# A graph attention kernel: E and the normed rows turned by VectorE blocks and DMAs instead of TensorE

## The chip, the cores and the metric

One NeuronCore of one Trainium2 chip runs the whole kernel. The metric is the device time of one execution in microseconds. The kernel before took 1281.48 us as the median of three runs (1281.45 to 1281.96).

## The reference, cut to what matters

64 graphs of 128 nodes with 256 features. The input is layer-normed and clipped at zero, goes through three layers of attention over the graph's edges and a feed-forward network, and the input is added at the end.

```python
h = maximum(layernorm(x), 0)
for l in range(3):
    si = h @ attn_w[l, :256];  sj = h @ attn_w[l, 256:]
    scores = si[:, :, None] + sj[:, None, :] + attn_b[l]
    scores = where(scores >= 0, scores, 0.2 * scores)
    scores = where(mask, scores, -inf)            # mask = adjacency or the diagonal
    agg = einsum('bij,bjd->bid', softmax(scores), h)
    h = layernorm(h + agg, g1[l], beta1[l])
    ff = gelu(h @ W1[l] + b1[l]) @ W2[l] + b2[l]  # 256 -> 1024 -> 256
    h = layernorm(h + ff, g2[l], beta2[l])
return x + h
```

## The kernel before

**Items.** Four graphs make a group, there are 16 groups, and one layer of one group is an item: 48 items. They run in rounds of 12: layer 0 of four groups, layer 1 of the same four, layer 2. In an item, partitions are the 128 nodes, and the free dimension holds 4 graphs of 256 features (`xs`, a ring of three). The four graphs' nodes make 512 columns in the feed-forward network.

**Orders written by hand.** Each engine has a list of steps for the first items and a function `slot(s)` for the rest, which places the steps of several items: f = item s, b = s+1, a = s+2, d = s+3, p = s+4, t = s-1, o = s-2. Engines run their lists in order and wait on semaphores. DMAs are all issued by SP, in its own order.

**An item's path, by the names in the code.** Attention: `j_dots` and `i_dots` (VectorE, L606 and L624) make sj and si; sj goes to DRAM and comes back broadcast to all partitions (`send_sj`, `load_sj`) with the element order node, graph, so that one graph's row is read with 16 bytes between elements; `masked` (L645) takes the minimum of it and a penalty; `leaky` (ScalarE, L838) adds si and applies the slope; `minus_max` (VectorE, L656) reduces to the negated maximum; `exps` (ScalarE, L844) makes E, with its row sums. TensorE turns E with four transposes (`e_turn`, L993) into the PSUM tile `util`, ScalarE copies it to `ET` (`et_out`, L851), and `aggregate` (L962) multiplies: eight halves of fp32 matmuls, ET being the weights. `attend` (VectorE, L660) divides by the sum and adds the rows. `moments1`, `make_rstd("1")` (GpSimd) and `norm1` (VectorE, L677) norm them. TensorE turns the normed rows with 2 x 4 transposes (`z1_turn`, L980) into `util`, `h_high` (ScalarE, L832) applies gain and offset and rounds, `h_low` (VectorE, L683) keeps the rest.

Feed-forward: `ffn1(i, c)` (L930) makes chunk c of eight of the hidden rows, six matmuls of 512 columns into one of three PSUM banks (`hbank`): it needs `low` of three chunks before. `gelu_high(i, c)` (ScalarE) applies gelu and rounds, `low(i, c)` (VectorE, L538) keeps the rest in one of four buffers, `ffn2(i, c)` (L944) adds 12 matmuls of 256 columns to `acc`. `residual` (L544), `moments2`, `norm2` and, on GpSimd, `x_gamma` and `x_beta` make the next layer's rows. `h_gamma` and `h_beta` (GpSimd) make the residual's rows `hb`.

**PSUM.** Eight banks: three `hbank`, four `acc` (an item's two halves, for two items in turn; both aggregate and ffn2 write them, L138), one `util`, which e_turn and z1_turn hand round with et_out and h_low.

**Inputs.** During the items in front of a new layer 0 VectorE also takes the moments of the next input (`input_moments`, `input_shift`), ScalarE norms it (`first_x`), and VectorE makes the penalty.

Of the kernel before, what the change touches and what calls it, by code (L numbers as in the profile page):

```python
# [25 lines left out]
F32 = mybir.dt.float32  # L26
# [7 lines left out]
P = 128  # L34
GG = 4
# [11 lines left out]
LEAD = 3  # L47

# [3 lines left out]
def build(nc, x, adj, attn_w, attn_b, W1, b1, W2, b2, g1, beta1, g2, beta2, out):  # L52
# [19 lines left out]
    with ExitStack() as ctx:  # L72
# [27 lines left out]
        ET = sb("ET", [P, GG, P])  # L100
        sj_bc = sb("sj_bc", [P, P, GG])
        sj_dram = nc.dram_tensor("sj_dram", [2, P, GG], F32).ap()
# [8 lines left out]
        dots = sb("dots", [P, 2, GG])  # L111
        si = sb("si", [P, GG])
# [4 lines left out]
        nmr0 = sb("nmr0", [P, GG])  # L117
        st = {n: sb(f"st{n}", [P, GG, 6]) for n in "012"}
        mv = {n: sb(f"mv{n}", [P, GG, 2]) for n in "012"}
        ve = {n: sb(f"ve{n}", [P, GG]) for n in "012"}  # L120
        rstd = {n: sb(f"rstd{n}", [P, GG]) for n in "012"}
# [13 lines left out]
        acc = [psum(f"acc{i}", [P, HG, D]) for i in range(4)]  # L135
        util = psum("util", [P, TOK])

        def acc_of(i, h): return acc[2 * (i.q % 2) + h]  # L138
# [28 lines left out]
        zt_n = sem("zt_n")  # L167

# [13 lines left out]
        si_n = sem("si_n")  # L182
        pen_n = sem("pen_n")
        mask_n = sem("mask_n")
        negm_n = sem("negm_n")
        rden_n = sem("rden_n")
        nmr0_n = sem("nmr0_n")
        st_n = {n: sem(f"st{n}_n") for n in "012"}
# [30 lines left out]

        def x_of(i):  # L220
            return xs[:, i.q % XR]
# [28 lines left out]

        def wait_ring(eng, q):

            if q >= XR:
                eng.wait_ge(zt_n, KD * (q - XR + 1))
                eng.wait_ge(hgam_n, 2 * (q - XR + 1))
# [3 lines left out]
        def _(sp):  # L259
# [36 lines left out]
            def load_weights(n):  # L296
                l, w, h = halves[n]
# [4 lines left out]
            def send_sj(i):  # L302
                sp.wait_ge(dotj_n, i.q + 1)
                wait(sp, sj_in, 16 * (i.q - 2))
                sp.dma_start(sj_dram[i.q % 2], dots[:, 1]).then_inc(sj_sent, 16)

            def load_sj(i):
                sp.wait_ge(sj_sent, 16 * i.q)
# [3 lines left out]

            def slot(s):
                t, o, d, p = item(s - 1), item(s - 2), item(s + 3), item(s + 4)
                if p and p.l == 0:
                    load_xraw(p)
                if 6 <= s + 5 < len(halves):
                    load_weights(s + 5)
                if s == ITEMS - 4:
                    sp.wait_ge(x0_n, GG * NG)  # L320
                    sp.dma_start(xraw[:], group(x, NG - 1)).then_inc(last_in, 16)
                if o and o.l == L - 1 and o.q < ITEMS - 1:
                    for h in range(2):
                        gs = slice(h * HG, (h + 1) * HG)
                        sp.wait_ge(out_ready, 2 * o.g + h + 1)
                        sp.dma_start(group(out, o.g)[:, gs], xout[:, o.g % 2, gs]).then_inc(out_sent[o.g % 2], 16)
                if t and t.l == L - 1 and t.q < ITEMS - 1:
                    wait(sp, out_ready, 2 * t.g)
                    if t.g == 0:
                        sp.wait_ge(ln1_ready, 1)  # L330
                    sp.dma_start(xres[:], group(x, t.g)).then_inc(xres_in, 16)
                if p and p.l == 0:
                    load_adj(p)
                if d:
                    send_sj(d)
                    load_sj(d)

            load_xraw(item(0))
# [10 lines left out]
            load_xraw(item(2))  # L349
            load_adj(item(1))  # L350
            load_ln2_rows()
            load_attn_rows(False)
            load_weights(4)
            send_sj(item(1))
            load_sj(item(1))
            load_adj(item(2))
            load_weights(5)
            load_adj(item(3))
            load_xraw(item(3))
            send_sj(item(2))  # L360
# [747 lines left out]
```

## Time and profile before

| | us |
|---|---|
| median of three runs | 1281.48 |
| the profiled execution | 1281.6 |
| its span, first to last instruction | 1279.8 |
| TensorE busy | 1240.6 (97% of the span) |
| VectorE busy | 1110.3 (87%) |
| ScalarE busy | 917.7 (72%) |
| GpSimd busy | 652.5 (51%) |
| DMA engines | 14.4% of the span, mean 41 GB/s |

TensorE's granted clock is 0.997 of 2.4 GHz over the span. In the profile PE is TensorE's matmuls, PEld its weight loads, DVE VectorE, ACT ScalarE, POOL GpSimd, SPq the queue from which SP issues DMAs. Matmuls overlap, so the distance between two starts tells what one costs, not its duration.

### The profile page before, as it was taken

How to read it: one execution, taken by the hardware profiler on the slowest of the kernel's cores; microseconds unless marked ns; L12 is line 12 of the kernel's file. 1: busy time of each engine (PE TensorE's matmuls, PEld its weight loads, DVE VectorE, ACT ScalarE, POOL GpSimd, SP SyncE). 2: the span in 40 equal slices, each digit the busy share in tenths (PEclk: the TensorE clock that was granted, in tenths of full speed). 3: DMA queues.
4: the chain of work that ended last, by engine and by line, in shares of the span. 5: the costliest groups of instructions: out<-in, count | busy, mean ns of one | idle time of the engine just before them, and what ended most of it. 6: DMA issues, size and time to landing. Idle time of an engine off the chain costs nothing.

```text
span 1279.8 us, 23042 instructions
## 1 busy us (share of the span) xinstructions
PE 1240.6 (97%) x7877; PEld 1122.5 (88%) x7877; DVE 1110.3 (87%) x3331; ACT 917.7 (72%) x1754; POOL 652.5 (51%) x535
## 2 busy tenths in 40 slices
PE   3899999999999999999999999999999999999997
PEld 1799999988899999999889999999989899989996
DVE  7888888899998788889998888789999888888765
ACT  4777777677876776678777776777778766776663
POOL 1435553556555534554566445544666355435563
PEclk9999999999999999999999999999999999999998
DMA  7111111112220001011230000002321100000111
GB/s 248 53 33 43 26 26 34 34 51 66 67 67 10 10 10 17 10 34 51 75 100 26 9 18 10 9 10 43 99 75 42 34 10 9 10 17 26 26 41 58
DMA packets 52944, 52.31 MB, mean 41 GB/s; under 512 B 9272, under 2 KB 45148, under 8 KB 52828
## 3 DMA queue, kind: packets, MB, share of 16 engines
q1 hardware_dynamic: 52828, 50.85, 14.4%
q8 instruction: 62, 1.02, 0.3%
q14 instruction: 54, 0.44, 0.1%
HBM read 42.36 MB, written 8.48 MB: 40 GB/s over the span
## 4 chain that ended last, share of the span: by engine, by line
PE 77%; DVE 18%; ACT 2%; issue 2%; DMA 1%; POOL 0%; DVEq 0%; POOLq 0%
PE acc L955 35%; PE hbank L940 33%; PE acc L969 5%; DVE hid_lo L541 3%; PE util L990 3%; DVE xs L680 2%; PE util L1000 1%; DVE xs L667 1%; DVE st L528 1%; DVE st L674 1%; DVE ve L519 1%; DVE mv L517 1%; DVE st L562 1%; DVE junk L627 1%; DVE sc L654 1%
## 5 line engine op out<-in xcount | busy, mean ns | idle before, releaser
L955 PE MATMUL acc<-w2hi,hid_hi 128*128 128x256 f32 x1536 | 446.0, 290 | 0.0
L813 ACT ACTIVATE hbank<-hbank,vec 128x512 f32<-128x512 f32 x384 | 253.7, 661 | 266.5 <-PE hbank L940 262.0
L955 PE MATMUL acc<-w2hi,hid_lo 128*128 128x256 f32 x1536 | 434.9, 283 | 0.0
L955 PE MATMUL acc<-w2lo,hid_hi 128*128 128x256 f32 x1536 | 434.4, 283 | 0.0
L389 POOL TENSOR_TENSOR rstd<-ve,halfs 128x4 f32<-128x4 f32 x111 | 120.1, 1082 | 492.1 <-DVE ve L519 487.2
L940 PE MATMUL hbank<-ht_hi,w1hi 128*128 128x512 f32 x768 | 311.2, 405 | 2.8 <-DVE hid_lo L541 1.4
L955 PEld LDWEIGHTS acc<-w2hi,hid_hi 128*128 128x128 f32 x1536 | 293.8, 191 | 10.5
L940 PE MATMUL hbank<-ht_lo,w1hi 128*128 128x512 f32 x768 | 302.6, 394 | 0.0
L955 PEld LDWEIGHTS acc<-w2lo,hid_hi 128*128 128x128 f32 x1536 | 293.7, 191 | 8.8
L940 PE MATMUL hbank<-ht_hi,w1lo 128*128 128x512 f32 x768 | 300.8, 392 | 0.0
L955 PEld LDWEIGHTS acc<-w2hi,hid_lo 128*128 128x128 f32 x1536 | 293.5, 191 | 0.0
L541 DVE TENSOR_TENSOR hid_lo<-hbank,hid_hi 128x512 fp32r<-128x512 f32 x384 | 257.5, 683 | 26.5 <-ACT hid_hi L819 24.7
L819 ACT CAST hid_hi<-hbank 128x512 fp32r<-128x512 f32 x384 | 225.6, 587 | 13.7 <-PE acc L955 1.7
L409 POOL TENSOR_TENSOR hb<-xs,ln_rows 128x512 f32<-128x512 f32 x96 | 128.9, 1343 | 87.2 <-DVE xs L680 87.2
L940 PEld LDWEIGHTS hbank<-ht_hi,w1lo 128*128 128x128 f32 x768 | 144.7, 188 | 32.6
L940 PEld LDWEIGHTS hbank<-ht_hi,w1hi 128*128 128x128 f32 x768 | 145.7, 190 | 25.6 <-DVE ht_lo L685 2.1
L940 PEld LDWEIGHTS hbank<-ht_lo,w1hi 128*128 128x128 f32 x768 | 145.9, 190 | 19.9
L685 DVE TENSOR_TENSOR ht_lo<-util,ht_hi 128x512 fp32r<-128x512 f32 x96 | 66.2, 689 | 95.1 <-ACT ht_hi L836 95.1
L416 POOL TENSOR_TENSOR hb<-hb,ln_rows 128x512 f32<-128x512 f32 x96 | 124.5, 1298 | 0.0
L680 DVE TENSOR_SCALAR xs<-xs,mv,rstd 128x256 f32<-128x256 f32 x192 | 112.0, 646 | 1.0 <-POOL rstd L389 0.9
L829 ACT ACTIVATE util<-util,vec 128x512 f32<-128x512 f32 x96 | 72.4, 754 | 36.1 <-PE util L990 35.9
L426 POOL TENSOR_TENSOR xs<-xs,ln_rows 128x512 f32<-128x512 f32 x64 | 82.7, 1292 | 23.4 <-DVE xs L570 23.4
(76 smaller groups left out, 1740.3 us busy)
## 6 DMA issues: line engine op xcount, KB each, us to landing
sj_bc<-sj_dram SPq DMA_DIRECT2D x47, 256.0 KB, 3.9
xraw<-in_x_dram SPq DMA_DIRECT2D x16, 512.0 KB, 4.4
out_dram<-xout SPq DMA_DIRECT2D x32, 256.0 KB, 4.4
xres<-in_x_dram SPq DMA_DIRECT2D x15, 512.0 KB, 5.6
xout<-in_L_gnn_W_dram SPq DMA_DIRECT2D x10, 512.0 KB, 5.0
adji<-in_adj_dram SPq DMA_DIRECT2D x16, 256.0 KB, 2.9
ln_rows<-in_L_gnn_g_dram SPq DMA_DIRECT2D x2, 384.0 KB, 8.0
ln_rows<-in_L_gnn_beta_dram SPq DMA_DIRECT2D x2, 384.0 KB, 7.6
```

The costliest lines, as they stand in the source:

```text
L389: pool.tensor_tensor(rstd[n][:], ve[n][:], halfs[:], ALU.pow).then_inc(rstd_n[n], 1)
L409: pool.tensor_tensor(hb[:, i.q % 2, gs], x_of(i)[:, gs], rows_of(ln1_rows[:, 0], i.l), ALU.mult).then_inc(hgam_n, 1)
L416: pool.tensor_tensor(t, t, rows_of(ln1_rows[:, 1], i.l), ALU.add).then_inc(hb_n, 1)
L426: pool.tensor_tensor(t, t, rows_of(ln2_rows[:, 0], i.l), ALU.mult).then_inc(gam_n, 1)
L541: dve.tensor_tensor(hid_lo[:, k % HID], hbank[k % HB][:], hid_hi[:, k % HID].bitcast(F32), ALU.subtract).then_inc(lo_n, 1)
L680: dve.tensor_scalar(x_of(i)[:, g], x_of(i)[:, g], mv["1"][:, g, 0:1], rstd["1"][:, g:g + 1], ALU.subtract, ALU.mult).then_inc(z1_n, 1)
L685: dve.tensor_tensor(ht_lo[:, i.q % 2, m], util[:], ht_hi[:, i.q % 2, m].bitcast(F32), ALU.subtract).then_inc(htlo_n, 1)
L813: act.activation(hbank[k % HB][:], hbank[k % HB][:], ACT.Gelu, bias=b1c(i.l, c)).then_inc(gelu_n, 1)
L819: act.copy(hid_hi[:, k % HID], hbank[k % HB][:]).then_inc(hi_n, 1)
L829: act.activation(util[:], util[:], ACT.Identity, bias=beta1c(i.l, m), scale=g1c(i.l, m)).then_inc(ht_n, 1)
L940: mm = pe.matmul(hbank[k % HB][:], w[:, i.l, m, at_c], v[:, i.q % 2, m], start=m == 0 and n == 0, stop=m == KD - 1 and n == 2)
L955: mm = pe.matmul(to, v[:, k % HID, of_g], w[:, i.l, c], start=c == 0 and n == 0 and g % HG == 0, stop=c == C - 1 and n == 2, skip_group_ch ...
```

## The change

For all items but the first two, E is turned by one VectorE operation that transposes blocks of 32x32 in place of the four TensorE transposes (`turn_e`), written to DRAM (`send_e`) and read back by four DMAs that put the blocks in their places (`move_e`); the normed rows likewise (`turn_z`, `send_z`, `move_z`), so `h_out` reads the SBUF tile `zt`. Pieces are 512 bytes. `ET` has the graph as its innermost dimension, so aggregate reads its weights with 16 bytes between elements. norm1 goes from VectorE to ScalarE, with its shift made by VectorE (`shift1`). minus_max no longer reduces E's scores: masked, now one operation for each graph, returns the maximum, from which two operations on 128x4 make the exponent's offset. add_bias goes (the offset is the start value of i_dots), input_shift is one operation instead of four, the variance's small operation goes to GpSimd. Aggregation gets two banks of its own (`mix`), ffn2 two (`acc`). All lists of steps are in another order; aggregate(a), for one, stands ahead of ffn1(b,0) instead of behind ffn1(b,2).

```diff
-        acc = [psum(f"acc{i}", [P, HG, D]) for i in range(4)]
+        acc = [psum(f"acc{i}", [P, HG, D]) for i in range(HG)]
+        mix = [psum(f"mix{i}", [P, HG, D]) for i in range(HG)]
...
+            def send_e(i):
+                if i.q < BY_PE:
+                    return
+                sp.wait_ge(te_n, moved(i.q))
+                wait(sp, et_in, MOVES * (moved(i.q) - 1))
+                sp.dma_start(e_dram, te[:].rearrange("p b t g -> p (b t g)")).then_inc(e_sent, 16)
+
+            def move_e(i):
...
+                sp.wait_ge(e_sent, 16 * moved(i.q))
+                sp.wait_ge(agg_n, 2 * i.q)
+                for b in range(NQ):
+                    sp.dma_start(ET[b * QD:(b + 1) * QD].rearrange("p a t g -> p a (t g)"),
+                                 e_dram.rearrange("(a p) (b f) -> b p a f", a=NQ, b=NQ)[b]).then_inc(et_in, 16)
+
+            def send_z(i):
...
+                sp.dma_start(z_dram, tz[:].rearrange("p c g t -> p (c g t)")).then_inc(z_sent, 16)
+
+            def move_z(i):
...
+                sp.wait_ge(z_sent, 16 * moved(i.q))
+                sp.wait_ge(ht_n, KD * i.q)
+                for b in range(NQ):
+                    sp.dma_start(zt[b * QD:(b + 1) * QD].rearrange("p m a g t -> p m a (g t)"),
+                                 z_dram.rearrange("(a p) (m b f) -> b p m a f", a=NQ, b=NQ, m=KD)[b]).then_inc(zt_in, 16)
...
# SP's slot
+                if b:
+                    send_z(b)
+                if a:
+                    send_e(a)
+                if b:
+                    move_z(b)
+                if a:
+                    move_e(a)
+                if t and t.l == L - 1:
+                    load_xres(t)
+                if o and o.l == L - 1:
+                    send_out(o, 1)
+                load_weights(s + 6)
+                if d:
+                    send_sj(d)
+                    load_sj(d)
...
# VectorE
-                dve.tensor_tensor(sc[:], pen[:, i.g % PENS], row, ALU.min).then_inc(mask_n, 1)
+                for g in range(GG):
+                    last = dve.tensor_tensor_reduce(sc[:, g], pen[:, i.g % PENS, g], row[:, g], 1.0, -BIG, ALU.add,
+                                                    ALU.max, msj[:, g:g + 1])
+                last.then_inc(mask_n, 1)
...
+            def turn_e(i):
...
+                dve.transpose(te[:].rearrange("p b i g -> p b g i"), sc[:].rearrange("p g (b j) -> p b g j", j=QD)).then_inc(te_n, 1)
+
+            def turn_z(i):
...
+                dve.transpose(tz[:], x_of(i).rearrange("p g (c j) -> p c g j", j=QD)).then_inc(tz_n, 1)
...
# ScalarE
+            def norm1(i):
+                act.wait_ge(nmr1_n, i.q + 1)
+                for g in range(GG):
+                    act.activation(x_of(i)[:, g], x_of(i)[:, g], ACT.Identity, bias=nmr1[:, g:g + 1],
+                                   scale=rstd["1"][:, g:g + 1]).then_inc(z1_n, 1)
...
# TensorE
-                    pe.wait_ge(y1_n, GG * (i.q + 1))
+                    wait(pe, y2_n, 2 * i.q)
...
-                    mm = pe.matmul(acc_of(i, h)[:, g % HG], ET[:, g], x_of(i)[:, g],
+                    mm = pe.matmul(mix_of(i, h)[:, g % HG], ET[:].rearrange("p a i g -> p (a i) g")[:, :, g], x_of(i)[:, g],
```

The new orders of a slot, by the names of the steps (those with p only where p is of layer 0, add_input, load_xres and send_out only for layer 2):

```
TensorE: ffn1(f,3) ffn2(f,0) ffn1(f,4) ffn2(f,1) ffn2(f,2) ffn1(f,5) ffn1(f,6) ffn2(f,3) ffn2(f,4) ffn1(f,7)
         aggregate(a,0) aggregate(a,1) ffn2(f,5) ffn1(b,0) ffn1(b,1) ffn2(f,6) ffn2(f,7) ffn1(b,2)
VectorE: turn_z(b) moments2(t) low(f,2) turn_e(a) input_moments(p) norm2(t,0) norm2(t,1) low(f,3) penalty(p)
         low(f,4) low(f,5) low(f,6) input_shift(p) j_dots(d) h_low(b,0) i_dots(d) attend(a,0) h_low(b,1)
         attend(a,1) moments1(a) low(f,7) masked(d) low(b,0) minus_max(d) shift1(a) low(b,1)
         residual(f,0) residual(f,1)
ScalarE: gelu_high(f,2) exps(a) gelu_high(f,3..6) h_high(b,0) h_high(b,1) gelu_high(f,7) first_x(p)
         gelu_high(b,0) gelu_high(b,1) leaky(d) norm1(a)
GpSimd:  h_gamma(b,1) make_rstd("2",t) make_rstd("0",p) x_gamma(t,0) x_beta(t,0) x_gamma(t,1) add_input(t,0)
         x_beta(t,1) make_rstd("1",a) h_beta(f,1) h_beta(b,0) add_input(t,1) h_gamma(a,0)
```

## Rows read from the trace of the kernel before

**Rows 1.** Busy time of each engine by stretch: start:end, length, busy, clock, DMA.
```profile
61.13:1270.11 1208.98, 1205.91 (x7721) 1096.00 (x7720) 1055.31 (x3141) 880.76 (x1680) 632.80 (x511) 1.00 0.13 35
...
sum 1279.80, PE 1240.58 PEld 1122.45 DVE 1110.27 ACT 917.72 POOL 652.54; mean PE 310.14 PEld 280.61 DVE 277.57 ACT 229.43 POOL 163.14
```

**Rows 2.** The chain of waits in order of time, one item: start, us, what.
```profile
502.75 2.75 PE hbank L940 x12
505.50 0.44 PE util L1000 x4
...
507.33 1.73 PE acc L969 x8
...
520.31 0.44 PE util L990 x4
...
524.01 4.32 PE acc L955 x36
```

**Rows 3.** Busy time by stretch (PE, PEld, DVE, ACT, POOL), two items.
```profile
509.28:534.86 25.58, 25.58 (x167) 23.29 (x166) 21.36 (x65) 18.25 (x35) 12.49 (x11) 1.00 0.08 11
...
637.18:662.76 25.58, 25.17 (x163) 22.68 (x162) 25.28 (x78) 19.57 (x39) 15.78 (x13) 1.00 0.28 80
```

**Rows 4.** VectorE's instructions in order of time: start, us, line, operation.
```profile
509.12 1.66 DVE L667 SCALAR_TENSOR_TENSOR xs<-acc,rden,xs 128x256 f32<-128x256 f32 x4
510.70 0.73 DVE L570 TENSOR_SCALAR xs<-xs,mv,rstd 128x256 f32<-128x256 f32 x2
511.34 0.69 DVE L541 TENSOR_TENSOR hid_lo<-hbank,hid_hi 128x512 fp32r<-128x512 f32 x1
511.94 1.40 DVE L674 BATCH_NORM_STATS2 st<-xs 128x6 f32<-128x256 f32 x4
...
513.79 0.29 DVE L519 TENSOR_SCALAR ve<-mv 128x4 f32<-128x4 f32 x1
...
515.24 1.10 DVE L654 TENSOR_TENSOR sc<-pen,sj_bc 128x512 f32<-128x512 bf16 x1
516.26 2.35 DVE L680 TENSOR_SCALAR xs<-xs,mv,rstd 128x256 f32<-128x256 f32 x4
```

**Rows 5.** ScalarE's instructions in order of time.
```profile
500.21 1.28 ACT L848 ACT_TABLE_LOAD   x1
501.51 0.41 ACT L848 ACTIVATE sc<-sc,negm 128x128 f32<-128x128 f32 x1
...
503.18 1.28 ACT L813 ACT_TABLE_LOAD   x1
...
505.17 0.59 ACT L819 CAST hid_hi<-hbank 128x512 fp32r<-128x512 f32 x1
...
520.79 0.75 ACT L829 ACTIVATE util<-util,vec 128x512 f32<-128x512 f32 x1 [0.59 <-PE util L990]
521.57 0.59 ACT L836 CAST ht_hi<-util 128x512 fp32r<-128x512 f32 x1
522.05 1.28 ACT L842 ACTIVATE sc<-sc,si 128x128 f32<-128x128 f32 x4
```

**Rows 6.** Groups by line (count, busy us, mean ns), and one instruction of ScalarE.
```profile
L969 PEld LDWEIGHTS acc<-xs,ET 128*128 128x128 f32 x384 | 73.6, 192 | 13.4 <-ACT ET L854 1.9
...
L510 DVE TENSOR_TENSOR w1lo<-xout,w1hi 128x1024 fp32r<-128x1024 f32 x6 | 7.3, 1218 | 0.7 <-ACT w1hi L808 0.7
...
L654 DVE TENSOR_TENSOR sc<-pen,util 128x512 f32<-128x512 bf16 x1 | 0.7, 683 | 0.0
...
610.34 2.09 ACT L862 ACTIVATE xs<-xraw,nmr,rstd 128x256 f32<-128x256 f32 x4
```

**Rows 7.** DMAs: KB, median us to landing; landing of out_dram; issue ns.
```profile
adji<-in_adj_dram SPq DMA_DIRECT2D x16, 256.0 KB, 2.9
...
DMA to landing us min/median/max: 2.1/4.4/5.7
...
L305 SPq DMA_DIRECT2D sj_dram<-dots x47: 319/320/339, 26.5 to 1196.7; - x47
```

## What I expect of the change

> **What bounds the kernel now.** I read the busy time by stretch first: from 61.13 to 1270.11 us TensorE is idle for 3.07 us only, and over the whole span it is busy 1240.58 of 1279.80 us, so 39.2 us of idle time lie almost wholly at the two ends [rows 1]. Then the chain of waits in order of time: in the steady part it runs through TensorE alone, without a wait [rows 2]. One item takes a period of 25.58 us: 8 chunks of the first product (2.75 us for two, so 1.38 each), 8 of the second (4.32 us for three, 1.44 each), one aggregation (1.73), and three groups of four transposes at 0.44 us, one for E and two for the normed rows [rows 2]. Then the busy time per item: VectorE has 21.4 of 25.58 us in most items, but 25.3 of 25.58 in the items during which the next inputs are also normed; there TensorE loses 0.4 us [rows 3]. So what TensorE saves is time saved, as long as VectorE (in four items of each twelve it is full) and the chains through the other engines let it.
>
> **What goes from TensorE.** For 46 of 48 items (the first two keep them) 3 x 0.44 = 1.32 us of transposes go: the period falls to 24.26 us, and 46 x 1.32 = 60.7 us in all. The profiled execution took 1281.6 us, 1.8 over its span, and agrees with the median of 1281.48. So the floor is 1281.6 - 60.7 = 1220.9 us, if nothing else stalls and the two ends stay as they are.
>
> **VectorE.** Out go: norm1, four operations in 2.35 us, where the same operation in norm2 takes 0.73 for two [rows 4] (so about 0.8 us of it is waiting beside GpSimd); the reduction for the maximum (512 elements, as the 0.6 us of low) becomes two operations of four elements; the tensor_scalar of the variances (0.29) twice or three times, and add_bias, of the same size [rows 4]. That is 2.35 + 0.6 + 0.6 + 0.2 = 3.8 us. In come two block transposes, of 512 and 1024 elements a partition. No row shows a block transpose on VectorE. Nearest are low (512 elements, 0.60 from start to start) and the 1024-element subtraction (1.22) [rows 4, 6]; from above I take twice these. A gain is excluded, since the operations are new. I take 0.8 + 1.2 = 2.0, near the lower end, since other operations here go by element count and only the write of the small one is strided; the upper end is 3.6. masked becomes four operations with an accumulator read: its strided form took 1.10 against 0.68 with a dense operand [rows 4, 6], and three more starts make it 1.3, between 1.1 and 2.0. shift1 and the two small operations of minus_max come to 0.6. Net: -3.8 + 2.0 + 0.2 + 0.6 = -1.0 us (up to +1.3 by the upper ends). A normal item has 20.4 of 24.26 us, an item with inputs about 24.3 of 24.26. VectorE is therefore the bound in the latter.
>
> **ScalarE** gets norm1, four operations in 2.09 us like first_x [rows 6], and loses the 0.6 us copy of E. It has 18.3 to 19.6 us an item now [rows 3], so some 21 of 24.26: room, but its place in the queue counts. GpSimd gets the small variance operations; at 12.5 to 15.8 us [rows 3] it has room.
>
> **The new chains.** Set zero at the start of ffn1(f,3) in a slot. The bound is the loop that starts when aggregate(a) ends at 15.8: reciprocal and half of attend (0.95), h_low (0.6), other half (0.8), moments1 (1.85), low (0.6), masked (1.3) on VectorE; leaky (1.28), norm1 (2.1) on ScalarE: 9.5 us. Behind norm1 in ScalarE's queue stand gelu_high (1.3), a table load, exps, a table load (1.28 + 1.67 + 1.28), gelu_high again (1.3), then low(f,3) (0.6): 7.4 us. Only then may ffn1(f,6) start, since three PSUM banks carry the hidden rows; to the next end of aggregate it is 1.38 + 2.88 + 1.38 + 1.73 = 7.4 us [rows 2, 4, 5]. Sum 24.3, with four handovers of up to 0.1 us 24.3 to 24.7, against 24.26 for TensorE. I take 24.4: +0.15 us in 34 normal items, 5 us. norm1 so ends 1.0 us into the next slot; behind it turn_z ends at 2.2, exps at 5.3 (1.0 + 1.3 + 1.28 + 1.67), turn_e at 6.1, low(f,3) at 8.3. In the 12 items with inputs, input_moments (1.85, like moments1) now stands between turn_e and norm2 in front of low(f,3): turn_e ends at 6.1, then 1.85, norm2 1.3, low 0.6: 9.9 instead of 8.3. With the 0.15 that is 1.7 us each, 20 us. attend, penalty, the moved dots and the merged shift lie elsewhere and are hidden by waits for gelu or for aggregate.
>
> **The own banks.** Aggregation gets two banks and ffn2 two instead of four taken in turn. ffn2(f,0) then waits for residual of the item before, which by the same clock ends at about 24.8, 0.5 us into the slot, and is wanted at 1.38. The 0.9 us of slack hides it; in items with inputs some 0.7 is left. The PSUM tile that et_out and the transposes held is no longer handed round.
>
> **E by DMA.** turn_e ends near 6.1, aggregate wants E at 14.1: 8.0 us. SP must write 256 KB (landing in 2.1 to 5.7 us, the least when nothing is in flight), then issue four pieces at 0.32 to 0.4 us each, the last of which lands like adji (256 KB in pieces of 512 bytes, 2.9) [rows 7]: 2.6 + 1.1 + 2.8 and some 0.2 for waits = 6.7. Hidden by 1.3 us. **The normed rows.** turn_z ends near 2.2; 512 KB out in 3.5, then four issues and the landing of 512 KB: 3.5 + 1.1 + 3.3 = 7.9, but send_e is queued ahead of move_z on SP and waits for turn_e until 6.1, so they are there at about 10.6; ScalarE turns to h_high at 11.3, when gelu_high(f,6) is done (ffn1(f,6) ends at 9.8). If they came later, h_high (0.75 + 0.59 for each half [rows 5]) with h_low between could start at 13.7 before ffn1(b,0) waits. On SP send_z and send_e now wait ahead of weights, xres and send_sj; send_sj wants its dots at 13 us, when SP has gone past, and load_sj is in before masked wants it at 20.
>
> **E's layout.** ET is now read as weights with 16 bytes from one element to the next. No row shows TensorE reading so. VectorE does in masked: 0.42 us more for 512 elements, 0.8 ns each [rows 4, 6]. Eight loads of 128 would cost 0 to 0.82 us an item. I take 0: a load takes 192 ns and a matmul of the aggregation 1.73 / 8 = 216 ns [rows 2, 6], loads run beside matmuls, and 0.1 us more for each may just fit. 
>
> **The start** is reordered: j_dots(i1) comes earlier, but aggregate(i2) must now go in front of ffn1(i0,7), with a DMA trip of its own. The first lets it pass two weight splits (1.22 each [rows 6]), attend and moments1 of i0, some 6 us; the second costs at most its trip, 6.7. I take 0, and ±6 for the range.
>
> **Sum:** 1220.9 + 5 + 20 = 1246 us.
>
> **The rivals.**
> 1. *The strided weights show.* Then 0.82 us an item on the loop, 46 x 0.82 = 38: 1284 us, no change within 0.2%. For it: masked's price. Against: the loads' cover. 0.08.
> 2. *VectorE is the bound everywhere*: block transposes at the upper ends put turn_z at 2.4 and turn_e at 1.2 in front of low(f,3), which comes 0.6 us later in every item: 46 x 0.6 = 28, 1274 us. For it: nothing but the lack of a row. 0.15. The Trainium skill (VectorE: DVE Perf Modes, Rules for kernel authors) advises TensorE for a 128x128 transpose whose result may be in PSUM, and 311 ns on VectorE for a bf16 one (The three transpose paths); twelve make 3.7 us, an estimate, which is this rival. No run here shows it.
> 3. *The DMA trips become the loop, and it is slower than before.* The trip of the normed rows has 11.5 us before ffn1 waits, from 2.2 to 13.7. Nearest rows from above are 5.7 us for 256 KB out, so up to 8.5 for 512, and 6.8 back with the issues: 15.3, which is 3.8 too long each item: 1246 + 175 = 1421 us. It decides from 11.5 us; from 12.3 it is slower than before (0.8 x 46 = 36). For it: 4.4 as the median landing of 256 KB out [rows 7]. Against: that median has other transfers in front of it, and 2.1 is what a free queue needs. 0.12.
> 4. *The loop closes with no loss and inputs fit*: 1221 to 1230. 0.12.
>
> The forecast itself (1232 to 1262) has 0.53.
>
> **How the numbers follow.** The range of 1222 to 1275 holds the forecast, rival 4 and nearly all of rival 2. About 0.2% is what a measurement here tells from no change. Faster: 0.53 + 0.12 + 0.15 and a little of rival 1 = 0.82. Within 0.2%: 0.05 (rival 1). Slower: 0.13, rival 3 and the upper side of rival 1.
>
> **What would show it.** Items of 24.3 to 24.5 us between inputs and near 26 with them; TensorE's idle time before ffn1(f,6), released by hid_lo. Block transposes near 0.8 and 1.2 us. Weight loads of the aggregation still near 192 ns and its eight matmuls in 1.73: if 2.5, rival 1. TensorE waiting at the aggregation for ET's DMA, or at ffn1(b,0) for ht_lo behind a late zt: rival 3. The prediction would be wrong above all if a DMA trip is longer than 8 us for E or 11.5 for the rows, or if the start is longer by more than 6 us.

## The result, and the profile after

The changed kernel takes 1343.3 us as the median (1336.6 to 1347.2), against 1281.7 for the kernel before on the same chip: ratio 1.047, interval 1.043 to 1.052. It is slower, where 1246 was forecast. The profiled execution took 1336.55 us, with a span of 1334.8.

The stretch that stood first of before, and one item without and one with inputs (start:end, length, busy time of PE, PEld, DVE, ACT, POOL, clock, DMA share, GB/s):

```profile
61.13:1270.11 1208.98, 1125.62 (x6841) 1000.02 (x6840) 1094.39 (x3193) 922.68 (x1770) 642.77 (x588) 1.00 0.31 92
...
508.74:534.63 25.89, 24.86 (x154) 22.20 (x154) 23.05 (x69) 19.81 (x39) 13.08 (x13) 1.00 0.24 72
645.05:673.87 28.82, 25.20 (x154) 22.15 (x154) 27.25 (x80) 21.77 (x43) 17.41 (x17) 1.00 0.40 129
```

TensorE was idle for 3 us of this stretch before [rows 1] and is idle for 83 now. An item without inputs takes 25.89 us where 25.58 stood [rows 3], and 24.4 was forecast; one with inputs 28.8 where 25.6 to 26.4 stood (the first is the one of [rows 3]), and 26 was forecast. VectorE is busy for 23.05 and 27.25 us of them, not for 20.4 and 24.3. TensorE did lose its transposes (25.58 us busy in an item before, 24.86 now); VectorE's busy time grew by 1.7 us an item where a fall of 1.0 was forecast.

VectorE in order of time, from the end of one item into the next (the counterpart of [rows 4]), then GpSimd and ScalarE in the same stretch:

```profile
504.61 0.66 DVE L768 SCALAR_TENSOR_TENSOR below<-msj,dots 128x4 f32<-128x4 f32 x1
505.30 1.22 DVE L771 SCALAR_TENSOR_TENSOR negm<-below 128x4 f32<-128x4 f32 x1
506.44 0.15 DVE L808 SCALAR_TENSOR_TENSOR nmr<-mv,rstd 128x4 f32<-128x4 f32 x1
506.51 0.68 DVE L648 TENSOR_TENSOR hid_lo<-hbank,hid_hi 128x512 fp32r<-128x512 f32 x1
...
508.74 1.25 DVE L786 STREAM_TRANSPOSE tz<-xs 128x1024 f32<-128x1024 f32 x1 [0.35 <-ACT xs L987]
...
512.86 1.12 DVE L779 STREAM_TRANSPOSE te<-sc 128x512 f32<-128x512 f32 x1 [0.60 <-ACT sc L1002]
513.82 2.27 DVE L677 TENSOR_SCALAR xs<-xs,mv,rstd 128x256 f32<-128x256 f32 x4
516.02 1.31 DVE L648 TENSOR_TENSOR hid_lo<-hbank,hid_hi 128x512 fp32r<-128x512 f32 x2
```
```profile
503.69 2.81 POOL L521 TENSOR_TENSOR hb<-hb,ln_rows 128x512 f32<-128x512 f32 x2
...
514.55 1.39 POOL L531 TENSOR_TENSOR xs<-xs,ln_rows 128x512 f32<-128x512 f32 x1 [1.43 <-DVE xs L677]
516.02 1.28 POOL L539 TENSOR_TENSOR xs<-xs,ln_rows 128x512 f32<-128x512 f32 x1
```
```profile
504.12 1.28 ACT L994 ACTIVATE sc<-sc,dots 128x128 f32<-128x128 f32 x4
506.63 2.08 ACT L987 ACTIVATE xs<-xs,nmr,rstd 128x256 f32<-128x256 f32 x4 [1.23 <-DVE nmr L808]
```

Look first at the two small operations of minus_max: four elements each, 0.66 and 1.22 us. Both lie beside h_beta on GpSimd (503.69 to 506.50, two operations), and the second ends when h_beta does. shift1, behind them, takes 0.15, and norm1 has waited 1.23 us for it. norm2 takes 2.27 us for four operations, the second pair beside x_gamma. low(f,3) then starts 0.6 us after its input (ScalarE's cast ended at 515.43), and TensorE waits 0.91 us for it:

```profile
516.75 0.50 PE L1104 MATMUL hbank<-ht_hi,w1hi 128*128 128x512 f32 x1 [0.91 <-DVE hid_lo L648]
```

The chain of waits in order of time (start, us, what), one item, which ran through TensorE alone before [rows 2], shows the same places (issue is time in which the engine waited for nothing that the profile shows; here it lies inside negm's 1.22 us):

```profile
504.69 0.59 DVE below L768
...
505.30 0.04 DVE negm L771
...
505.76 0.68 issue
506.44 0.16 DVE nmr L808
506.63 0.51 ACT xs L987
507.13 1.57 ACT xs L987 x3
...
511.49 1.35 ACT sc L1002 x7
512.86 1.12 DVE te L779
513.99 2.11 DVE xs L677 x4
516.10 0.61 DVE hid_lo L648
516.75 1.67 PE hbank L1104 x6
```

In an item with inputs i_dots is hit too; two of its four operations take 1.46 and 1.49 us beside add_input and x_beta (L562, L539), the other two 0.47:

```profile
630.78 1.46 DVE L736 CUSTOM_DVE_ANT_0 junk<-xs,attn_rows,attn_bias 128x256 bf16<-128x256 f32 x1
632.17 1.49 DVE L736 CUSTOM_DVE_ANT_0 junk<-xs,attn_rows,attn_bias 128x256 bf16<-128x256 f32 x1
633.59 0.47 DVE L736 CUSTOM_DVE_ANT_0 junk<-xs,attn_rows,attn_bias 128x256 bf16<-128x256 f32 x1
```
```profile
630.68 1.27 POOL L562 TENSOR_TENSOR xout<-xout,xres 128x512 f32<-128x512 f32 x1 [1.83 <-DMA xres<-in_x_dram]
631.91 1.47 POOL L539 TENSOR_TENSOR xout<-xout,ln_rows 128x512 f32<-128x512 f32 x1
```

The DMAs, to be set beside [rows 7] (pieces, KB, median us to landing):

```profile
z_dram<-tz SPq DMA_DIRECT2D x46, 512.0 KB, 2.6
zt<-z_dram SPq DMA_DIRECT2D x184, 128.0 KB, 2.8
...
e_dram<-te SPq DMA_DIRECT2D x46, 256.0 KB, 2.0
ET<-e_dram SPq DMA_DIRECT2D x184, 64.0 KB, 2.1
```

ScalarE waited for zt twice, 2.0 us in all; TensorE never for an ET that came by DMA. VectorE waited for rows that GpSimd's wide operations make (j_dots for x_beta) for 2.8 us in all, so it is not the arrival of GpSimd's results that costs here.

### The profile page after: what moved, and what is told of

It reads as the page before. It is cut to its first block, busy times and chain, and to the rows that moved or that the text cites. A ratio compares the mean times of both kernels' runs of the same rounds, so it can differ in the third digit from the quotient of the medians.

```text
span 1334.8 us, 23057 instructions
## 1 busy us (share of the span) xinstructions
PE 1212.2 (91%) x7325; PEld 1074.4 (80%) x7325; DVE 1175.0 (88%) x3454; ACT 992.0 (74%) x1900; POOL 696.9 (52%) x648
## 4 chain that ended last, share of the span: by engine, by line
DVE 49%; ACT 23%; issue 11%; PE 9%; DMA 1%; POOL 1%; DVEq 0%; SPq 0%
PE hbank L1104 6%; ACT xs L987 6%; DVE hid_lo L648 6%; DVE xs L795 5%; DVE sc L760 5%; DVE junk L736 5%; ACT sc L1002 5%; ACT L1002 4%; ACT hbank L953 4%; DVE st L802 4%; DVE junk L727 4%; DVE ht_lo L814 4%; DVE xs L677 4%; DVE te L779 3%; PE acc L1119 2%
## 5 line engine op out<-in xcount | busy, mean ns | idle before, releaser
L492 POOL TENSOR_SCALAR ve<-mv 128x4 f32<-128x4 f32 x111 | 27.4, 247 | 452.1 <-DVE mv L627 452.1
L514 POOL TENSOR_TENSOR hb<-xs,ln_rows 128x512 f32<-128x512 f32 x96 | 121.9, 1291 | 62.8 <-DVE xs L662 44.2
L987 ACT ACTIVATE xs<-xs,nmr,rstd 128x256 f32<-128x256 f32 x192 | 99.7, 590 | 47.8 <-DVE nmr L808 47.8
L521 POOL TENSOR_TENSOR hb<-hb,ln_rows 128x512 f32<-128x512 f32 x96 | 132.6, 1400 | 0.2
L975 ACT ACTIVATE util<-zt,vec 128x512 f32<-128x512 f32 x92 | 72.3, 786 | 75.0 <-DVE ht_lo L814 73.0
L494 POOL TENSOR_TENSOR rstd<-ve,halfs 128x4 f32<-128x4 f32 x111 | 115.4, 1040 | 9.3
L531 POOL TENSOR_TENSOR xs<-xs,ln_rows 128x512 f32<-128x512 f32 x64 | 85.6, 1338 | 41.1 <-DVE xs L677 41.1
```

Source lines behind the costliest of these rows:

```text
L494: pool.tensor_tensor(rstd[n][:], ve[n][:], halfs[:], ALU.pow).then_inc(rstd_n[n], 1)
L514: pool.tensor_tensor(hb[:, i.q % 2, gs], x_of(i)[:, gs], rows_of(ln1_rows[:, 0], i.l), ALU.mult).then_inc(hgam_n, 1)
L521: pool.tensor_tensor(t, t, rows_of(ln1_rows[:, 1], i.l), ALU.add).then_inc(hb_n, 1)
L531: pool.tensor_tensor(t, t, rows_of(ln2_rows[:, 0], i.l), ALU.mult).then_inc(gam_n, 1)
L975: act.activation(util[:].rearrange("p (g a t) -> p a g t", g=GG, a=NQ), zt[:, m], ACT.Identity, bias=beta1c(i.l, m), scale=g1c(i.l, m)).th ...
L987: act.activation(x_of(i)[:, g], x_of(i)[:, g], ACT.Identity, bias=nmr1[:, g:g + 1], scale=rstd["1"][:, g:g + 1]).then_inc(z1_n, 1)
```

## The experiments

Two theories follow from these rows: GpSimd's operations of 512 elements hold VectorE's up while both run (A), or VectorE simply has too much work, in a bad order. Each text in quotes below was written before its run. Ratios are to the kernel before on the same chip, which took 1281.4 to 1281.7 us in every batch. The last column gives the period of typical single items of the profiled execution, as the distance between the starts of two aggregations. The changed kernel's own runs lie 10 us apart (1336.6 to 1347.2) and the profiled one is the fastest, so a few us against it are not told apart.

| kernel | us | ratio, interval | items without / with inputs, us |
|---|---|---|---|
| before | 1281.5 | | 25.58 / 25.6–26.4 |
| after | 1343.3 | 1.047, 1.043–1.052 | 25.89 / 28.8 |
| a1_shift_first | 1321.8 | 1.030, 1.027–1.033 | 25.0–25.7 / 28.9 |
| a2_beta_early | 1345.8 | 1.051, 1.048–1.053 | 26.33 / 29 |
| a3_dense_weights | 1330.9 | 1.039, 1.037–1.041 | 25.6–25.7 / 28.6 |
| a4_low3_first | 1360.3 | 1.061, 1.060–1.063 | 26.1 / 29.5–30.9 |
| b1_shift_and_max | 1353.6 | 1.057, 1.055–1.059 | 26.25 / 28.3 |
| b2_small_gpsimd | 1247.4 | 0.973, 0.972–0.975 | 24.35 / 25.4 |
| b3_e_on_tensor | 1334.1 | 1.041, 1.039–1.042 | 25.6–25.7 / 28.8 |
| b4_e_on_tensor_order | 1361.7 | 1.063, 1.058–1.067 | 26.2–27.4 / 27.6–29.4 |
| n1_before_small | 1275.3 | 0.995, 0.994–0.997 | 25.58 / 25.58 |
| n2_h_small | 1280.6 | 0.999, 0.998–1.000 | 24.55 / 28.0 |
| d1_gpsimd_apart | 1273.7 | 0.994, 0.992–0.995 | 24.71 / 26.5 |
| d2_apart_moments_late | 1270.9 | 0.992, 0.990–0.993 | 24.71 / 26.24 |
| e1_apart_e_tensor | 1266.3 | 0.988, 0.987–0.990 | 24.67 / 25.68 |
| e2_apart_dense | 1258.1 | 0.982, 0.980–0.983 | 24.45 / 25.97 |
| e3_apart_no_z2_wait | 1265.7 | 0.988, 0.986–0.990 | 24.56 / 26.35 |

Not all items are of these two kinds. Means over the 44 periods from the fourth aggregation to the last, in us, by what lies in them, and the rest of the span:

| kernel | first 6 (weights still being split) | 18 around new inputs | the other 20 | rest of the span |
|---|---|---|---|---|
| before | 25.58 | 25.92 | 25.58 | 148.1 |
| after | 26.41 | 28.02 | 25.95 | 153.0 |
| b2_small_gpsimd | 24.97 | 25.33 | 24.37 | 153.4 |
| n2_h_small | 25.09 | 26.87 | 24.56 | 153.6 |
| d2_apart_moments_late | 25.60 | 25.93 | 24.71 | 154.6 |
| e3_apart_no_z2_wait | 25.04 | 25.96 | 24.56 | 155.2 |

**a1_shift_first.** VectorE's list of a slot:

```diff
                     masked(d)
+                if a:
+                    shift1(a)
                 if b:
                     low(b, 0)
                 if d:
                     minus_max(d)
-                if a:
-                    shift1(a)
```

> The changed kernel with one step moved on VectorE: shift1(a) stands in front of low(b,0) and minus_max(d) instead of behind them. Theory (a collision): in the changed kernel the two small two-source operations of minus_max take 0.66 and 1.22 us because GpSimd's two h_beta operations run then, shift1 comes behind them, and norm1 on ScalarE waits 1.2 us with nothing else to do, on the loop that sets the period. Then shift1 comes out of their shadow, norm1's wait nearly goes, and 46 items x 1.2 us = 55 us go: some 1285 us, normal items 24.7 us instead of 25.89. Rival (VectorE's work is the bound, 27.1 of 30 us busy): the order within an item makes no difference, 1330 to 1345 us.

Norm1's waits fell from 47.8 to 8.9 us, but only 21 us of the expected 55 were gained. shift1 now took 1117 ns on average and minus_max's two operations 454 and 295: the one that comes first beside h_beta is held longest. TensorE then waited 31 us in all for residual, a second way, to which the prediction had given 0.9 us of slack: ffn2 has one pair of banks now, so the next item's ffn2(f,0) waits for residual.

**a2_beta_early** puts h_beta(f,1) and h_beta(b,0) ahead of make_rstd("1",a) on GpSimd.

> The changed kernel with only GpSimd's order changed: h_beta(f,1) and h_beta(b,0) in front of make_rstd(1,a), in what was GpSimd's idle time. VectorE's order is as before. Theory (a collision): minus_max's two operations fall to some 0.2 us each, shift1 follows at once, norm1's wait goes: 55 us less, some 1285 us; some may come back where h_beta now meets the dots (up to 1.3 us an item, which VectorE's idle time there may hide), so between 1285 and 1320. Rival (VectorE's or ScalarE's own work is the bound): 1330 to 1345 us and the operations of minus_max as long as they were.

No gain: 1345.8 us lies among the changed kernel's own runs, not at 1285 to 1320. minus_max's operations fell to 286 and 163 ns as expected, but j_dots rose from 418 to 728, and TensorE waited 50 us for ht_lo where it had waited 13. The overlap had moved, not gone.

**a3_dense_weights.** te and ET with 32 elements of a graph side by side; the aggregation multiplies by rows of E in a wrong order, the work is the same:

```diff
-        ET = sb("ET", [P, NQ, QD, GG])
-        te = sb("te", [P, NQ, QD, GG])
+        ET = sb("ET", [P, NQ, GG, QD])
+        te = sb("te", [P, NQ, GG, QD])
```

> The changed kernel with te and ET dense in the innermost dimension: turn_e writes without steps, aggregate reads its weights without steps. The four blocks then belong to other graphs than they should, so the aggregation multiplies by wrong rows of E; all sizes, DMAs and waits are the same. Theory: weight loads fall from 324 to 192 ns and turn_e from 1.13 to about 0.68 us; the aggregation becomes 0.12 us shorter (1.85 to 1.73), and turn_e's 0.35 us count in front of low(f,3): 46 x 0.45 = 20 us less, some 1320 us. Rival (both are hidden): the durations fall, the time stays at 1336 to 1347 us.

Weight loads fell from 324 to 192 ns and turn_e from 1129 to 711, and the whole by 12 us, where 20 were expected. The layout is a small part of the loss.

**a4_low3_first** puts low(f,3) and input_moments(p) between norm2(t,0) and norm2(t,1), and make_rstd("0",p) behind x_gamma(t,0).

> The changed kernel with low(f,3) on VectorE right behind norm2(t,0), in front of input_moments and norm2(t,1), and on GpSimd make_rstd(0) behind x_gamma(t,0). Theory: TensorE's waits for hid_lo (51 us in all, 0.9 us in a normal item and 1.7 in one with inputs) stand in front of ffn1(f,6), and low(f,3) waits for norm2 though its input is ready 0.6 us before, in items with inputs 2 us before: 34 x 0.5 + 12 x 2 = 41 us less, some 1300 us. Rival (VectorE is the bound where inputs are normed): 17 us less at most, from the normal items alone, some 1325 us.

Slower by 17 us, where a gain of 41 was expected. x_beta comes later, into j_dots (418 to 477 ns) and masked (497 to 593), and ScalarE's wait for ht_lo went from 73 to 110 us. Why it is so much was not taken apart.

**b1_shift_and_max** is a1 with minus_max(d) behind both residuals.

> The changed kernel with shift1(a) ahead of low(b,0) on VectorE, as in a1_shift_first, and minus_max(d) moved from ahead of low(b,1) to the end of the list, behind both residuals. a1 showed that TensorE then waits for residual (the first ffn2 of the next item) instead of for hid_lo. Theory A (two loops of equal length: one through shift1, norm1 and exps to ffn1(f,6), the other through leaky or masked and low to residual and ffn2(f',0); GpSimd's operations hold minus_max's two small ones and shift1 on the way of both): residual ends 0.6 to 1.2 us earlier, items without inputs fall from a1's 25.35 to 24.7 to 25.0, items with inputs stay near 28.5, about 1305 us. Theory B (VectorE's queue is simply full, the order only moves the wait): no gain over a1, 1318 to 1325 us. Theory C (the exponent needs its offset early, so putting minus_max last makes exps late and turn_e with it): slower than a1, 1330 or more.

Slower than a1 by 32 us. The time is theory C's, its mechanism is not: VectorE waited for exps 1.5 us in all. minus_max landed beside h_gamma (751 and 1126 ns for its two operations), in front of turn_z. b4_e_on_tensor_order, the same on top of b3, was slower than b3 by 28 us in the same way (1163, 1128 and 798 ns for the three small operations); it was expected at 1265 to 1280.

**b2_small_gpsimd** is the decisive one: VectorE's program stays, and GpSimd's wide operations become small. In h_gamma, h_beta, x_gamma, x_beta and add_input alike:

```diff
+            def wide(i):
+                return D if i.q < 2 else 2
...
-                pool.tensor_tensor(t, t, rows_of(ln2_rows[:, 0], i.l), ALU.mult).then_inc(gam_n, 1)
+                pool.tensor_tensor(t[:, :, 0:wide(i)], t[:, :, 0:wide(i)], rows_of(ln2_rows[:, 0], i.l)[:, :, 0:wide(i)], ALU.mult).then_inc(gam_n, 1)
```

> The changed kernel, with its order untouched, in which GpSimd's five kinds of wide operation (h_gamma, h_beta, x_gamma, x_beta, add_input) work on 2 of 256 features from the third item on: this leaves out the residual rows' gain and offset, the layer norm's gain and offset and the added input for the other 254. Every wait and signal stays. Theory A (GpSimd's wide operations hold back VectorE's operations while they run, most of all the small ones of minus_max and shift1 and the two-source ones): items without inputs fall from 25.89 to 24.3 to 24.6, those with inputs from 28.8 to 26.0 to 26.8, norm1 stops waiting for its shift, the penalty falls back from 1321 to about 700 ns, and the whole takes 1245 to 1265 us. Theory B (VectorE's own work, its block transposes and its list order set the time, GpSimd only runs beside it): over 1310 us with items of 25.5 or more. Theory C (both, in equal parts): 1280 to 1300 us.

96 us fall away with VectorE's program unchanged, as theory A says; items with inputs went further than it said, to 25.4. Groups of VectorE by line (count, busy us, mean ns), first of after, then of b2 (three line numbers further):

```profile
L736 DVE CUSTOM_DVE_ANT_0 junk<-xs,attn_rows,attn_bias 128x256 bf16<-128x256 f32 x192 | 97.5, 563 | 0.0
L677 DVE TENSOR_SCALAR xs<-xs,mv,rstd 128x256 f32<-128x256 f32 x128 | 70.1, 609 | 0.0
L771 DVE SCALAR_TENSOR_TENSOR negm<-below 128x4 f32<-128x4 f32 x48 | 39.5, 822 | 1.7
L768 DVE SCALAR_TENSOR_TENSOR below<-msj,dots 128x4 f32<-128x4 f32 x48 | 30.0, 625 | 0.1
L746 DVE SCALAR_TENSOR_TENSOR pen<-adji,diag 128x512 bf16<-128x512 int32 x16 | 21.1, 1321 | 0.0
```
```profile
L739 DVE CUSTOM_DVE_ANT_0 junk<-xs,attn_rows,attn_bias 128x256 bf16<-128x256 f32 x192 | 81.2, 478 | 0.0
L680 DVE TENSOR_SCALAR xs<-xs,mv,rstd 128x256 f32<-128x256 f32 x128 | 43.7, 404 | 0.0
L774 DVE SCALAR_TENSOR_TENSOR negm<-below 128x4 f32<-128x4 f32 x48 | 7.8, 163 | 1.6
L771 DVE SCALAR_TENSOR_TENSOR below<-msj,dots 128x4 f32<-128x4 f32 x48 | 9.2, 192 | 0.1
L749 DVE SCALAR_TENSOR_TENSOR pen<-adji,diag 128x512 bf16<-128x512 int32 x16 | 10.9, 683 | 0.0
```

What did not change although it runs beside a wide operation: low (678 to 680 ns; one lies beside h_beta), turn_z (1245 both, beside h_gamma) and the moments of the residual (403 to 402, partly beside h_gamma). So held are those with both inputs in SBUF, and norm2, which has one; not held are low, with one input in PSUM, the transpose and the moments. turn_e ran beside no wide operation in these items, so its 1129 ns in both say nothing on this. TensorE is busy for all of an item without inputs in b2:

```profile
502.68:527.04 24.36, 24.36 (x154) 22.39 (x153) 20.75 (x69) 19.78 (x39) 4.47 (x12) 1.00 0.26 77
```

The Trainium skill (SBUF — State Buffer, Who interferes with whom) states it so: a VectorE instruction with two SBUF inputs, or one in a mode that uses both ports, which tensor_scalar can enter, is held by a GpSimd instruction that reads SBUF, or holds it: the first to start has the shared ports for its whole length. The rows above agree, the four-element operation held for 1.22 us until h_beta ended most plainly.

**n1_before_small** is the same cut in the kernel before.

> The kernel before, with GpSimd's wide operations cut to 2 of 256 features from the third item on as in b2_small_gpsimd (leaves out most of the gains, offsets and the added input). Theory A (GpSimd holds VectorE back in the kernel before too, but beside waits for TensorE, where it costs nothing; TensorE is the bound): 1276 to 1281 us, while norm1 falls from 2.35 to about 1.3 us for its four operations. Theory B (the kernel before gains as much as the changed one did from cutting GpSimd, so the cut says nothing about the change): under 1265 us.

Only 6 us, just under what theory A gave: the items with inputs fall from 25.6–26.4 to 25.58, and norm1 from 646 to 415 ns a piece. So the overlap was there before, behind a full TensorE.

**n2_h_small** cuts h_gamma and h_beta alone.

> The changed kernel with only h_gamma and h_beta cut to 2 of 256 features (leaves out most of the residual rows' gain and offset); x_gamma, x_beta and add_input stay whole. Theory A (minus_max and shift1, held by h_beta and h_gamma, are what lengthens an item without inputs; norm2 and i_dots, held by the x operations, add mostly in items with inputs): items without inputs 24.6 to 25.0, those with inputs 27.3 to 28.2, 1275 to 1290 us. Theory B (the x operations in front of low(f,3) cost most): items without inputs 25.3 or more, over 1305 us.

63 of the 96 us go with those two; cutting x_gamma, x_beta and add_input as well takes the other 33 (these were not cut alone). By the table of means, of the 56 us between the two profiled executions 28 lie in the 20 late periods without inputs, 21 in the 18 around inputs and 8 in the first 6. Of the 32 from n2 to b2, 28 lie around inputs.

**b3_e_on_tensor** turns E by TensorE again, with a dense ET (its waits for the PSUM tile are left out of the lines).

```diff
-                    turn_e(a)
...
                     ffn2(f, 2)
+                if a:
+                    e_turn(a)
...
                     gelu_high(f, 3)
+                if a:
+                    et_out(a)
```

> The changed kernel with E turned by TensorE again (four transposes behind ffn2(f,2), copied by ScalarE behind gelu_high(f,3), with a dense ET as weights); the normed rows still go by VectorE blocks and DMA, aggregation keeps its own banks, all other steps keep their places. VectorE loses turn_e (1.13 us an item), TensorE gets 0.44 us back, ScalarE 0.6 us, weight loads fall from 324 to 192 ns. Theory A (the item is bound by VectorE's chain in front of low(f,3), and turn_e of 1.13 us stands in it): items without inputs near 25.0, those with inputs near 27.7, about 1295 us. Theory B (the ScalarE part of the loop binds: the copy adds 0.6 us to it and gives back what turn_e saves): 1315 to 1335 us. Theory C (E's trip through DRAM was itself in the way): under 1285 us.

9 us of gain, hardly more than the scatter of the changed kernel, and 39 us more than theory A gave. The time is at the end of theory B's range, but TensorE's waits for hid_lo, where that loop ends, fell from 53 to 3 us; those for residual rose from 19 to 37 and those for ht_lo from 13 to 27. So taking 1.13 us off VectorE is worth little while minus_max (628 and 877 ns), which stands in front of residual, is held.

**d1_gpsimd_apart** leaves nothing out and changes only when GpSimd works (the prologue also gets h_beta(i1,1); conditions are left out of the lines):

```diff
                     h_gamma(b, 1)
+                    h_beta(b, 0)
                     make_rstd("2", t.q)
                     make_rstd("0", p.g)
+                        pool.wait_ge(z2_n, GG * (t.q + 1))
                     x_gamma(t, 0)
                     x_beta(t, 0)
                     x_gamma(t, 1)
-                    add_input(t, 0)
                     x_beta(t, 1)
+                    pool.wait_ge(htlo_n, KD * (b.q + 1))
+                    h_beta(b, 1)
+                    add_input(t, 0)
                     make_rstd("1", a.q)
-                    h_beta(f, 1)
-                    h_beta(b, 0)
+                    pool.wait_ge(nmr1_n, a.q + 1)
                     add_input(t, 1)
                     h_gamma(a, 0)
```

> The changed kernel with only GpSimd's list of steps changed, nothing left out: the residual rows' operations for item b all come in one slot (h_gamma(b,1), h_beta(b,0) behind norm1, h_beta(b,1) behind h_low(b,1)), x_gamma(t,0) waits for both halves of norm2(t), and what follows make_rstd1(a) waits for shift1(a). So the wide operations lie beside turn_z, moments2, the low steps and moments1, and not beside norm2, minus_max and shift1, which b2_small_gpsimd suggests they hold back. Theory A (it is the overlap in time that costs, not the work): items without inputs fall from 25.89 to 24.4 to 24.9, those with inputs from 28.8 to 27.0 to 28.0, 1265 to 1285 us, level with the kernel before. Theory B (wherever the wide operations lie, they take the same from VectorE, as a2_beta_early made it look): 1320 us or more.

Theory A holds: 69.6 us less than after, by the list of one engine with the same work in it, and faster than the kernel before by 0.6%.

**d2_apart_moments_late** also puts input_moments(p) behind norm2(t,1) and make_rstd("0",p) behind x_gamma(t,1).

> d1_gpsimd_apart with input_moments(p) behind norm2(t,1) instead of ahead of norm2(t,0), and make_rstd0(p) behind x_gamma(t,1): in items with inputs norm2 and the x operations no longer move 1.9 us later into the dots. Items without inputs are the same program as d1. Theory A: items with inputs gain 0.5 to 1.5 us against d1, 6 to 18 us in all. Theory B (an item with inputs is limited by VectorE's sum of work, where the order makes no difference): within 3 us of d1.

2.8 us, below what theory A said (6 to 18); items with inputs gain 0.27 us. VectorE in d2, the counterpart of the first timeline of after:

```profile
511.50 0.15 DVE L772 SCALAR_TENSOR_TENSOR below<-msj,dots 128x4 f32<-128x4 f32 x1
511.68 0.16 DVE L775 SCALAR_TENSOR_TENSOR negm<-below 128x4 f32<-128x4 f32 x1
511.76 0.16 DVE L812 SCALAR_TENSOR_TENSOR nmr<-mv,rstd 128x4 f32<-128x4 f32 x1
...
519.37 1.30 DVE L681 TENSOR_SCALAR xs<-xs,mv,rstd 128x256 f32<-128x256 f32 x4
...
526.07 0.42 DVE L731 CUSTOM_DVE_ANT_0 junk<-xs,attn_rows 128x256 bf16<-128x256 f32 x1 [0.61 <-POOL xs L539]
```

**e3_apart_no_z2_wait** is d2 without the wait on z2_n.

> d2_apart_moments_late without GpSimd's wait for the second half of norm2(t): x_gamma(t,0) starts 0.6 us earlier and lies beside two of the four norm2 operations. Theory A (the wide operation holds them until it ends, 0.6 to 1.2 us, in front of low(f,3)): items without inputs rise from 24.71 to 25.0 to 25.6, norm2's mean from 385 ns to 500 or more, 1285 to 1305 us. Theory B (j_dots, which waits 0.61 us for x_beta in d2, is what sets the item, so x 0.6 us earlier is a gain): 24.4 to 24.6, 1262 to 1268 us.

norm2 is held as theory A said, 629 ns instead of 385, but the item got shorter, 24.56, as theory B said: low(f,3) had slack for it, and j_dots no longer waited 0.61 us for x_beta. In d2 the chain of waits of such an item runs through GpSimd's four x operations (520.75 to 526.04); in e3 it runs through TensorE alone. The chain in d2:

```profile
520.75 1.29 POOL xs L531
522.11 1.29 POOL xs L539
...
526.07 0.19 DVE junk L731
```

A held operation costs only where something waits for it. This is 1.2% under the kernel before, and with e1 below (0.6 us apart, within the scatter of both) the fastest that leaves nothing out and computes the same.

**e1_apart_e_tensor** is d2 with b3's edit, **e2_apart_dense** d2 with a3's.

> d2_apart_moments_late with E turned by TensorE and copied by ScalarE again, as in b3_e_on_tensor, and dense weights. Theory A (without the overlap TensorE nearly sets an item without inputs, and VectorE an item with inputs): TensorE gets 0.44 us back, items without inputs 24.7 to 24.9; items with inputs lose turn_e's 1.13 us, from 26.24 to 25.2 to 25.6, so 1260 to 1270 us, at least level with d2. Theory B (moving E off TensorE is a gain even so): items without inputs over 25.0, 1275 us or more.

> d2_apart_moments_late with te and ET dense, as in a3_dense_weights (the aggregation multiplies by rows of E in the wrong order). Theory A (the strided weight loads are hidden, what the layout costs is turn_e's 0.4 us on VectorE, which counts in items with inputs): items with inputs fall by 0.3 to 0.5 us, those without by 0 to 0.2, 1260 to 1267 us. Theory B (the weight loads show on TensorE, 0.1 to 0.5 us an item): items without inputs also fall by 0.3 or more, under 1258 us. Theory C (both are hidden): within 2 us of d2.

e1 is 4.6 us faster than d2: TensorE then sets an item without inputs (25.58 - 2 x 0.44 = 24.70, measured 24.67), those with inputs gain 0.56. So moving E off TensorE, once the overlap is thinned, gains nothing in this layout. e2, which keeps E on VectorE and DMA but densely, is 8 us faster than e1; its rows of E are in the wrong order, so this shows what the strided layout takes and is no kernel to use. e2 fell between its theories: 0.26 us an item, 12.9 in all. Half of an item's gain is seen on TensorE: from the aggregation's first matmul to the next ffn2 1.66 us in d2 (502.81 to 504.47), 1.54 in e2. The rest is turn_e's 0.42 us; how they add up to 0.26 was not separated.

## Why the prediction was wrong, step by step

1. **What bounds the kernel, and the floor.** This step was right. TensorE was full, and without its transposes an item is 24.26; b2 reached 24.35 with TensorE busy for all of it.
2. **The price of VectorE's operations** is the step that failed, in VectorE's sum and again in the loop. Each operation was costed by the duration of a row like it, without asking what GpSimd runs at its new place. The sum has shift1 and the two small operations of minus_max at 0.6 us together; the loop has no term for them at all, and gives no reason, and has norm2 at 1.3 us. The small ones took 0.15 to 0.16 each where they ran alone (d2), but 0.66 and 1.22 beside h_beta, and norm2 took 2.27 beside x_gamma. VectorE was busy for 23.05 us of an item without inputs where 20.4 was forecast; with GpSimd's operations made small it is 20.75 (b2). The prediction had seen the effect itself ("so about 0.8 us of it is waiting beside GpSimd", of norm1) and booked it as a gain of moving norm1. b2 gives back 96 of the 97 us between forecast and result.
3. **The loop.** As added up, masked is followed at once by leaky and norm1 on ScalarE. In the trace minus_max and shift1 run beside leaky but end 1.2 us after it, and norm1 waits 1.23 us; further on norm2 makes low(f,3) 0.6 us late. The two lengthen the loop by 1.8 us, and the item is 1.5 longer than forecast, so the other terms were some 0.3 too large together. With GpSimd small norm1's wait goes, and the item is 24.35 against 24.4 forecast; there TensorE sets it, not the loop. The second loop, through residual and the one pair of banks (0.9 us of slack given), was walked once and not with held operations in it: TensorE waited 18.6 us in all for residual in after, 31 in a1.
4. **Items with inputs**: 26 was forecast; 25.4 came in b2 and 28.8 in after. More items are touched than the 12 counted: 18 periods around the inputs are longer than the rest, 28.02 us on average, and hold 48 of the 88 us between the profiled executions of after and b2. The first six are longer too (26.41, and 24.97 in b2); there VectorE still splits weights, a term that the prediction put at nothing. The row of VectorE nearly full was read rightly; the penalty (750 to 1321 ns) and i_dots (two of four held) were not foreseen.
5. **Block transposes**: 0.8 and 1.2 were taken, 1.13 and 1.25 measured, within the ends given; 711 ns for E when it is written densely, so 0.42 us is the price of its strided write.
6. **The DRAM trips** were hidden, as forecast, though the four issues that read back took 2.56 us for the normed rows and 1.97 for E where 1.1 was taken. Rival 3, which held the chance of slower, did not happen; the kernel is slower for another reason, to which the prediction gave no rival and no chance.
7. **Strided weights** (rival 1): a load went from 192 to 324 ns, of which 0.13 us an item shows on TensorE, not 0 and not 0.82.
8. **The ends**: 0 ± 6 was taken. The aggregation of the fourth item starts at 93.04 instead of 95.42, and behind the start of the last (1274.8 instead of 1227.2) come 60.0 us instead of 52.6: 5.0 us longer in all, in range, with a gain at the start and a loss at the end.

With step 2 taken out by b2 the rest of the sum stands: 1247.4 measured, 1246 forecast. Part of this closeness is luck: an item with inputs was taken 0.6 us too long, the first six 0.6 too short, and the ends are 5.3 us longer than before.

## What to carry to other kernels

When an operation is added to or moved on VectorE, look up in the trace what GpSimd runs at that place: four elements can cost 1.2 us beside a wide GpSimd operation. Give short operations on the critical path a place where GpSimd is idle or works beside VectorE operations that read PSUM, and do the same with GpSimd's own list; here GpSimd's list alone was worth 70 us (d1), and 78 with input_moments moved and one wait taken out (e3), with no work removed. A stall seen in a row is not gone when its victim moves to another engine: look for who takes the place (shift1 in a1, j_dots in a2, minus_max in b1). And it costs only where something waits for the held operation: in the kernel before, behind a full TensorE, the same overlap was worth 6 us.

## What the runs showed of the hardware

- Who is held on VectorE beside a GpSimd tensor_tensor of 512 elements, in b2 against after: 128x4 operations with two SBUF inputs (163 ns on average, up to 1.22 us), tensor_scalar from SBUF to SBUF (404 to 609 ns on average), the products with accumulator (0.47 to 1.49 us), the penalty (683 to 1321 ns). Who is not: tensor_tensor with one input in PSUM (680 and 678), the block transpose of 1024 elements (1245 both), the moments (402 and 403).
- A block transpose of 1024 fp32 elements a partition on VectorE took 1245 ns, of 512 elements 711 when written densely and 1129 when written with 16 bytes between elements.
- A weight load of 128x128 fp32 read with 16 bytes between elements took 324 ns against 192, and cost 0.13 us for eight.
- Through DRAM in pieces of 512 bytes, from issue to landing: 2.0 us for 256 KB out and 2.1 for each of the four DMAs of 64 KB back; 2.6 for 512 KB out and 2.8 for each of four of 128 KB back. The four issues add 1.97 and 2.56 us. The waits for zt came to 2.0 us in after and to 9.7 at most (a4).
